# SyncE fetches one of 48 columns of source rows with single-row DMAs, and every edge pass gets six row buffers

## The chip, the cores and the metric

The kernel runs on one core of a Trainium2 chip. A core has five engines with an instruction stream each: TensorE (PE, with its weight loads as PEld), VectorE (DVE), ScalarE (ACT), GpSimd (POOL) and SyncE (SP), and 16 DMA engines that they share. SyncE computes nothing: it waits, works on registers and issues DMAs. The metric is device time in microseconds (us) from one launch, the median of several runs; lower is better. The kernel before took 13483.18 us (three runs, 13480.51 to 13506.48).

## The reference

A stack of four graph layers over 12,500 nodes and 200,000 edges, float32. Each layer takes rows of a node table by the source of every edge and reduces them over the edges that share a destination. Cut to what matters:

```python
def _transformer_conv(x, src, dst, edge_attr, ...):          # twice: passes c1, c2
    ke = k[src] + e
    score = jnp.sum(q[dst] * ke, axis=-1) / jnp.sqrt(...)
    smax = jax.ops.segment_max(score, dst, num_segments=n_nodes)
    a = jnp.exp(score - smax[dst])
    denom = jax.ops.segment_sum(a, dst, num_segments=n_nodes)
    out = jax.ops.segment_sum((a / denom[dst])[:, None] * (v[src] + e), dst, ...)

# three attention layers of 4 or 1 heads: passes c3 (with edge attributes), c4, c5
logits = leaky_relu(ax_s[:, row] + ax_t[:, col] + ae, 0.2)
w = jnp.exp(logits - seg_max[col].T)
out = segment_sum(w / denom[col] * x_proj[:, row], col)

z = h[src] + h[dst] + ef                                     # pass c6
mean, mean_sq = segment_sum(z, dst) / deg, segment_sum(z * z, dst) / deg
mx, mn = segment_max(z, dst), segment_min(z, dst)
```

## The kernel before, in words

Edges come sorted by destination. They are laid over 128 partitions, 1563 per partition (ET), so that one *column* is one edge of each partition, 128 edges in all. Sixteen columns (GW) are a *group*; there are 98 groups (NGRP), the last of 11 columns. Each of the six edge passes c1 to c6 goes once over all groups: `conv_edges` makes c1 and c2, `gat_edges` c3 to c5, `pna_edges` c6. Between the passes stand node stages (`n1` to `n5`, `f6`), and before them `begin`.

In every pass POOL fetches the source rows: for each column one indirect DMA takes 128 rows out of a node table in device memory, by the indices in column `srcs[:, g*GW+k]`, into the row buffer `y` (L741 in c1 and c2, L1767 in c3 to c5, L2200 in c6). A row is 256 bytes (`h_tab`, c1, c2, c6) or 288 bytes (`g_tab`, c3 to c5). The POOL code is written out in full, 1563 fetches to a pass; only the first 80 of c1 are issued in `begin` already (L415). `y` has six slots of a group each in c1 and c2 (NY = 6) and two in c3 to c6; before a group's fetches POOL waits until VectorE has read the group that had the slot (`weighted`, or `added` in c6). Slot 1 of six, where the short last group comes, counts its rows on two semaphores.

VectorE takes the groups in order. In c1 and c2 it spreads q over the edges with scans (L763), multiplies with the rows (L773, the first instruction that needs them), reduces, keeps running maxima, weighs the rows (L799, which frees the slot) and sums with scans (L806). In c3 to c5 the first reader is L1796, in c6 L2228. ScalarE makes exponentials, turns q and masks into scan order (L839, L841) and stores the summed rows.

SyncE issues what else is loaded. In c1 and c2, for each group, `operands` waits until the group two before it is weighted and its q turned (L715, L716), then issues `q_rows` (L706, 776 KB) and `edge_attrs` (L710, 256 KB in pieces of 128 bytes, 16 per partition). In c3 it issues the attributes of a group after the matmul that read the last ones (L1742), in c6 after `added` (L2179); in c4 and c5 it has nothing to do after the first load. Waits on each engine hold whatever stands behind them in that engine's own stream.

Of the kernel before, what the change touches and what calls it, by code (L numbers as in the profile page):

```python
# [19 lines left out]
I32 = mybir.dt.int32  # L20
ALU = mybir.AluOpType
# [3 lines left out]
P = 128  # L25
# [27 lines left out]
HALVED = (NGRP - 1) % NY  # L53
BLOCKS = [(c, min(8, NC - c)) for c in range(0, NC, 8)]
NBLOCK, NGOT, LAG = len(BLOCKS), 4, 3
assert NP_ >= N_NODES and EP >= N_EDGES and NBLK % 2 == 0 and NGRP % 2 == 0 \
    and EP % CH == 0 and GW // 2 < GL <= GW and NS > NC and NS % (2 * SC) == 0
# [44 lines left out]
def width(g):  # L102

    return GL if g == NGRP - 1 else GW

# [44 lines left out]
class Stage:  # L150
# [38 lines left out]
    def gather_halves(self, name, each):  # L189

        return [[self.dma(f"{name}{b}{part}", each - CUT * b * part) for part in range(2)] for b in range(2)]

    def row_slots(self, fills, cut=0):

        return [[self.dma(f"gathered_first_{slot}{part}", (8 if slot == HALVED else 16) * GW * n - cut * part)
                 for part in range(1 + (slot == HALVED))] for slot, n in enumerate(fills)]

# [13 lines left out]
def build(nc, a, out):  # L211
# [40 lines left out]

    def by_edge(t):
        return t[0:EP, :].rearrange("(p t) f -> p t f", p=P)
# [12 lines left out]
    def indexed(ap):  # L267
        return bass.IndirectOffsetOnAxis(ap=ap, axis=0)

# [30 lines left out]
    def begin(y, wq_t, bq, wk_t, bk, we_t):  # L300
# [4 lines left out]
        row_i, row = sb("row_i", [P, 1], I32), sb("row", [P, 1])  # L305
        node_i, node, upto = sb("node_i", [P, NS], I32), sb("node", [P, NS]), sb("upto", [P, NS])
# [26 lines left out]
        w_loaded, srcs_loaded = st.dma("w_loaded", 16 * len(loads)), st.dma("srcs_loaded", 16)  # L333
        ad_zeroed, h_stored, q_stored = st.dma("ad_zeroed", 16 * AD), st.dma("h_stored", 16), st.dma("q_stored0", 16)
        scattered = [st.dma(f"scattered{b}", 16 * sum(n for _, n in BLOCKS[b::2])) for b in range(2)]
        filled = [st.dma(f"zeros_stored{b}", 16 * len(range(b, NGRP, 4))) for b in range(4)]
        gathered = st.row_slots([1] * (NY - 1))
        chunk_got = st.dma_slots("chunk_got", 16 * (NS // 2))
# [10 lines left out]
            whole_t whole_pen""")  # L349

        with nc.Block(no_gpsimd_drain=True) as block:
            @block.sync
            def _(sp):
# [6 lines left out]
                sp.dma_start(prev_i[:], a["dst"][0:EP].rearrange("(p t) -> p t", p=P)).then_inc(dst_loaded.h, 16)  # L360
                sp.wait_ge(*zeroed(1))
# [19 lines left out]
                sp.dma_start(by_node(q_tab), q_rows[:]).then_inc(q_stored.h, 16)  # L381
                sp.wait_ge(*ad_zeroed(16 * AD))
# [191 lines left out]

            @block.tensor
# [94 lines left out]
    def conv_edges(tag, rows, first_y=None):  # L670
# [21 lines left out]
        gathered = st.row_slots([len(range(slot, NGRP, NY)) - (slot < ahead) for slot in range(NY)], CUT)  # L692
# [9 lines left out]
        with nc.Block(no_gpsimd_drain=True) as block:  # L702
            @block.sync
            def _(sp):
# [28 lines left out]
            def _(pool):  # L733

                nc.gpsimd.indirect_dma_start(q0[:], None, q_tab, indexed(dst0[:])).then_inc(q0_got.h, 16)
                for g in range(ahead, NGRP):
# [3 lines left out]
                    for k in range(width(g)):  # L740
# [9 lines left out]
            def _(v):  # L750
                def step(pc, slot, use):
# [18 lines left out]
                    for part in halves(gathered[slot], pc):  # L770
                        v.wait_ge(*part((use + (slot >= ahead)) * ((8 if slot == HALVED else 16) * GW) - missing(pc)))
# [928 lines left out]
    def gat_edges(tag, rows, bd=None):  # L1700
# [4 lines left out]
        y = st.sb("y", [P, 2, GW, TG])  # L1705
# [23 lines left out]
        gathered = st.gather_halves(f"gathered_{'first' if tag in ('c1', 'c2', 'c3') else 'later'}_", 8 * GW * HALF)  # L1729
# [8 lines left out]
        with nc.Block(no_gpsimd_drain=True) as block:  # L1738
            @block.sync
            def _(sp):  # L1740
# [5 lines left out]
                sp.dma_start(ad_raw[:], by_edge(ad_start)).then_inc(ad_loaded.h, 16)  # L1746
                if bd is not None:
                    for b in range(2):
                        edge_attrs(0, b, GW)
                    with sp.Fori(1, HALF - 1) as i:  # L1750
                        for b in range(2):
                            sp.wait_ge(*e_scored[b](i))
                            edge_attrs(i, b, GW)
# [5 lines left out]
            def _(pool):  # L1759
                nc.gpsimd.indirect_dma_start(g0[:], None, g_tab, indexed(dst0[:])).then_inc(g0_got.h, 16)  # L1760
                for g in range(NGRP):
                    b = g % 2
                    if g >= 2:
                        pool.wait_ge(*weighted[b](g // 2))
                        pool.nop(nofuse=True)
                    for k in range(width(g)):
                        nc.gpsimd.indirect_dma_start(y[:, b, k, :], None, g_tab, source(g, k))\  # L1767
                            .then_inc(gathered[b][k // H2].h, 16)
# [17 lines left out]
            def _(v):  # L1786
                def step(pc):
                    g, i, b, w = pc.n, pc.i, pc.b, pc.w
                    cols = bass.ds(pc.col, w)
                    ys = y[:, pc.slot, pc.lo:pc.lo + w]  # L1790
# [3 lines left out]
                    for part in halves(gathered[pc.slot], pc):  # L1794
                        v.wait_ge(*part(pc.load * (8 * GW) + 8 * GW - missing(pc)))
# [67 lines left out]
                with v.Fori(0, HALF - 1) as i:  # L1863
                    for b in range(2):
                        step(piece(i, b))
                for pc in LASTS:
                    step(pc)
# [277 lines left out]
    def pna_edges(tag, rows):  # L2145
# [4 lines left out]
        y, ea = st.sb("y", [P, 2, GW, D]), st.sb("ea", [P, 2, GW, D])  # L2150
# [16 lines left out]
        gathered = st.gather_halves(f"gathered_{'first' if tag in ('c1', 'c2', 'c3') else 'later'}_", 8 * GW * HALF)  # L2167
# [7 lines left out]
        with nc.Block(no_gpsimd_drain=True) as block:  # L2175
            @block.sync
            def _(sp):
# [3 lines left out]

                for b in range(2):
                    edge_attrs(0, b, GW)
                with sp.Fori(1, HALF - 1) as i:
                    for b in range(2):
                        sp.wait_ge(*added[b](i))
                        edge_attrs(i, b, GW)
# [5 lines left out]
            def _(pool):  # L2193
                for g in range(NGRP):
                    b = g % 2
# [434 lines left out]
```

## Time and profile before

| | |
|---|---|
| median of the runs | 13483.18 us |
| span of the profiled execution | 13480.4 us |
| POOL busy | 10010.5 us (74%) |
| DVE busy | 6813.4 us (51%) |
| ACT busy | 4134.7 us (31%) |
| source-row fetches | 9378 in six passes |

The profiled execution is its own run; its span leaves out what lies ahead of the first and behind the last instruction of the kernel, and is 2.8 us under the median of the runs. "Busy" leaves out the time between two instructions, in which POOL gets its next indirect DMA ready; that time is shown as "idle before", put down to "issue". DMA issues of SyncE aren't counted as busy, but the timeline shows each with its duration, under the engine name SPq. Lines L1 to L2629 are lines of the kernel before.

### The profile page before, as it was taken

What the parts mean: (1) busy time and instruction counts of PE and PEld (TensorE: products, weight loads), DVE (VectorE), ACT (ScalarE), POOL (GpSimd) and SP (SyncE); (2) the same over time, 40 slices, a digit from 0 to 9 for tenths busy, and PEclk for the clock granted to TensorE, in tenths of its full rate; (3) what the DMA queues carried; (4) which work ended last, traced back from release to release, by engine and by line L of the source; (5) the groups of instructions that cost most, each with busy time, mean ns of one, the idle gap of its engine ahead of it and who ended that gap; (6) DMA issues with size and microseconds to landing.
All of it is one profiled execution on the core that took longest, in us unless ns stands there. A gap on an engine that the chain in (4) does not pass through costs nothing. (4 is left out here: it accounts for less than half of the span.)

```text
span 13480.4 us, 46161 instructions
## 1 busy us (share of the span) xinstructions
PE 515.1 (4%) x1768; PEld 338.5 (3%) x1768; DVE 6813.4 (51%) x10542; ACT 4134.7 (31%) x4038; POOL 10010.5 (74%) x10585
## 2 busy tenths in 40 slices
PE   3000001100000300000010000000000000000001
PEld 1000000100000200000000000000000000000000
DVE  2787776477777433333333333343333335656566
ACT  4333333233333312222212222211111113666663
POOL 7777777777777677777777777777777776777775
PEclk9999999555555655555555555555555555555555
DMA  8444443344444222222212222222222222444443
GB/s 328 128 126 119 119 119 100 95 119 119 120 120 120 57 66 63 63 61 63 60 47 59 59 58 59 59 48 57 59 59 59 58 59 82 159 159 157 159 153 121
DMA packets 919562, 1312.58 MB, mean 97 GB/s; under 512 B 600892, under 2 KB 616404, under 8 KB 906113
## 3 DMA queue, kind: packets, MB, share of 16 engines
q0 software_dynamic: 341536, 381.76, 15.7%
q10 hardware_dynamic: 85680, 537.82, 10.2%
q1 hardware_dynamic: 492209, 391.76, 10.1%
q14 instruction: 123, 1.01, 0.0%
q8 instruction: 14, 0.23, 0.0%
HBM read 651.09 MB, written 659.48 MB: 97 GB/s over the span
## 5 line engine op out<-in xcount | busy, mean ns | idle before, releaser
L1767 POOL DMA_INDIRECT c_y<-g_tab,srcs x4689 | 4426.0, 944 | 1429.0 <-issue 1376.9
L2200 POOL DMA_INDIRECT c_y<-h_tab,srcs x1563 | 1474.8, 944 | 510.8 <-issue 466.5
L741 POOL DMA_INDIRECT c_y<-h_tab,srcs x1563 | 1474.9, 944 | 476.3 <-issue 476.3
L1796 DVE TENSOR_TENSOR c_s<-c_y,c_ad 128x64 f32<-128x64 f32 (+1 forms) x297 | 79.1, 266 | 3450.0 <-DMA c_y<-g_tab,srcs 3448.7
L741 POOL DMA_INDIRECT first_y<-h_tab,srcs x1483 | 1399.3, 944 | 452.9 <-issue 451.7
L1879 ACT ACTIVATE c_ex<-c_de 128x64 f32<-128x64 f32 (+1 forms) x297 | 67.4, 227 | 2321.1 <-DVE c_de L1827 2320.0
L1840 DVE TENSOR_TENSOR_SCAN c_acc<-c_r,c_w_in 128x1156 f32<-128x1156 f32 (+1 forms) x297 | 753.0, 2535 | 23.2
L763 DVE TENSOR_TENSOR_SCAN c_q_all<-c_mask,c_q_in 128x408 f32<-128x408 f32 (+2 forms) x792 | 734.0, 995 | 17.8 <-issue 10.5
L806 DVE TENSOR_TENSOR_SCAN c_acc<-c_r,c_w_in 128x408 f32<-128x408 f32 (+2 forms) x792 | 731.1, 986 | 8.2
L839 ACT ACTIVATE c_q_in<-c_q_raw 128x1552 f32<-128x1552 f32 (+1 forms) x198 | 596.2, 3011 | 195.8 <-DVE c_q_in L822 195.8
L1893 ACT ACTIVATE c_row<-c_acc 128x1088 f32<-128x1088 f32 (+1 forms) x297 | 617.7, 2080 | 0.0
L853 ACT ACTIVATE c_ex<-c_de 128x16 f32<-128x16 f32 (+1 forms) x198 | 37.1, 187 | 1842.2 <-DVE c_de L795 1842.2
L1833 DVE TENSOR_TENSOR c_w_in<-c_y,c_ex 128x1024 f32<-128x1024 f32 (+1 forms) x297 | 581.4, 1957 | 0.0
L867 ACT ACTIVATE c_row<-c_acc 128x1552 f32<-128x1552 f32 (+1 forms) x198 | 564.6, 2852 | 0.0
L2243 DVE TENSOR_TENSOR_SCAN c_acc_s<-c_mask,c_su 128x442 f32<-128x442 f32 (+2 forms) x495 | 477.5, 1031 | 121.5 <-ACT c_su L2325 121.5
L2228 DVE TENSOR_TENSOR c_su<-c_y,c_ea_ps 128x1024 f32<-128x1024 f32 (+1 forms) x99 | 184.7, 1866 | 663.4 <-DMA c_y<-h_tab,srcs 663.4
L1879 ACT ACT_TABLE_LOAD x96 | 123.2, 1283 | 1268.2 <-DVE c_de L1827 1268.2
L2249 DVE TENSOR_TENSOR_SCAN c_acc_m<-c_penm,c_mu 128x442 f32<-128x442 f32 (+2 forms) x495 | 474.8, 1024 | 0.0
L1892 ACT ACTIVATE c_row<-c_fm 128x64 f32<-128x64 f32 (+1 forms) x297 | 91.4, 308 | 1149.2 <-DVE c_acc L1840 1149.2
L2334 ACT ACTIVATE c_row<-c_acc_s 128x2048 f32<-128x2048 f32 (+1 forms) x99 | 374.1, 3779 | 141.9 <-DVE c_acc_s L2243 141.9
L2336 ACT ACTIVATE c_row<-c_acc_m 128x2048 f32<-128x2048 f32 (+1 forms) x99 | 374.3, 3781 | 85.2 <-DVE c_acc_m L2249 85.2
L773 DVE TENSOR_TENSOR c_prod<-c_y,c_q_all 128x1552 f32<-128x1552 f32 (+1 forms) x99 | 173.2, 1749 | 396.3 <-DMA c_y<-h_tab,srcs 396.3
(402 smaller groups left out, 6461.6 us busy)
## 6 DMA issues: line engine op xcount, KB each, us to landing
rows_d<-c_row ACTq DMA_DIRECT2D x97, 2048.0 KB, 6.9
rows_d<-c_row ACTq DMA_DIRECT2D x291, 576.0 KB, 2.9
rows_d<-c_row ACTq DMA_DIRECT2D x194, 784.0 KB, 3.4
c_q_raw<-q_start SPq DMA_DIRECT2D x194, 776.0 KB, 4.5
q_start<-first_y SPq DMA_DIRECT2D x97, 776.0 KB, 9.0
c_y<-g_tab,srcs POOLq DMA_INDIRECT x4689, 2.5
c_y<-h_tab,srcs POOLq DMA_INDIRECT x3126, 2.5
c_ea<-in_edge_attr SPq DMA_DIRECT2D x97, 512.0 KB
```

The source lines that it names most:

```text
L741: nc.gpsimd.indirect_dma_start(y[:, g % NY, k, 0:D], None, h_tab, source(g, k))\
L763: last = v.tensor_tensor_scan(flat(qs[:, lo:hi]), flat(mk[:, 0:hi - lo]), flat(q_cur[:, lo:hi]), 0.0, ALU.mult, ALU.add)
L806: last = v.tensor_tensor_scan(flat(ac[:, lo:hi]), flat(rr[:, 0:hi - lo]), flat(w_cur[:, lo:hi]), 0.0, ALU.mult, ALU.add)
L839: act.activation(narrow(q_in[:, pc.b], pc.w)[:, :, 1:pc.w + 1], q_raw[:, pc.slot, pc.lo:pc.lo + pc.w].rearrange("p t f -> p f t"), ACT.Copy)
L867: act.activation(row[:, b, 0:w, 0:F], narrow(acc[:, b], w)[:, :, 1:w + 1].rearrange("p f t -> p t f"), ACT.Copy).then_inc(row_ready[b].h, 1)
L1767: nc.gpsimd.indirect_dma_start(y[:, b, k, :], None, g_tab, source(g, k))\
L1833: v.tensor_tensor(w_heads[:, :, 0:JG, 1:w + 1], ys[:, :, 0:D].rearrange("p t (h j) -> p h j t", h=H), ex[:, :, 0:w].unsqueeze(2).to_broadc ...
L1840: v.tensor_tensor_scan(flat(ac), flat(rr), flat(w_cur), 0.0, ALU.mult, ALU.add).then_inc(summed.h, 1)
L1893: act.activation(row[:, b, 0:w, 0:F], narrow(acc[:, b], w)[:, :, 1:w + 1].rearrange("p f t -> p t f"), ACT.Copy).then_inc(row_ready[b].h, 1)
L2200: nc.gpsimd.indirect_dma_start(y[:, b, k, :], None, h_tab, source(g, k))\
L2243: last = v.tensor_tensor_scan(flat(ac_s[:, lo:hi]), flat(mk[:, 0:hi - lo]), flat(su_c[:, lo:hi]), 0.0, ALU.mult, ALU.add)
L2249: last = v.tensor_tensor_scan(flat(ac_m[:, lo:hi]), flat(pm[:, 0:hi - lo]), flat(mu_c[:, lo:hi]), 0.0, ALU.add, ALU.max)
```

## The change

Of every three groups the last column of the third (k = 15 of slots 2 and 5) is no longer fetched by POOL. SyncE fetches its 128 rows one by one. There are 32 such columns (NSYNC). A table `places_d` in device memory, made in `begin` from the sources by VectorE, holds the byte offsets of the rows, once for 256-byte rows and once for 288-byte rows. SyncE brings a column's 128 offsets into one row of a small SBUF tile `at`, reads them in pieces of 21 or 22 into registers (TENSOR_LOAD), and issues one DMA per row with the offset from a register. A column is cut in thirds (43, 43 and 42 rows); one third is issued for each group, behind that group's operands. `load_places` and `await_places` bring the next offsets in time; `whole_first` fetches the whole first column at the start of a pass, except in c1, where POOL has fetched groups 0 to 4 in `begin`. VectorE waits for a column's rows in `arrived`. In c3 to c6 the row buffer `y` grows from two slots to six, the loops are written over six groups instead of two, and SyncE gets such a loop in c4 and c5 too.

```diff
+EVERY, SYNC_K = NY // 2, GW - 1
+SYNC_SLOTS, NSYNC = [EVERY - 1, NY - 1], NGRP // EVERY
+THIRDS = [0, 43, 86, P]
+def by_pool(g):
+    return width(g) - (g % NY in SYNC_SLOTS)
+    class SyncRows:
+        def load_places(self, sp, n, b):
+            sp.dma_start(self.at[b:b + 1, :], places_d[bass.ds(n * 2 + b + self.table * NSYNC, 1), :])\
+                .then_inc(self.at_loaded.h, 16)
+        def await_places(self, sp, n, b):
+            sp.wait_ge(*self.at_loaded((n * 2 + b + 1 - self.first) * 16))
+        def third(self, sp, b, part):
+            lo, hi = THIRDS[part:part + 2]
+            mid = (lo + hi + 1) // 2
+            rows = self.tab.rearrange("n f -> (n f)").bitcast(U8)
+            for a_, z in ((lo, mid), (mid, hi)):
+                _, places = nc.values_load_multi_w_load_instructions(
+                    self.at[b:b + 1, a_:z], [mybir.EngineType.SP], min_val=0, max_val=(NP_ - 1) * 4 * self.width,
+                    skip_runtime_bounds_check_because="rows of src")
+                for p, place in zip(range(a_, z), places):
+                    sp.dma_start(self.y[p:p + 1, SYNC_SLOTS[b], SYNC_K, 0:self.width].bitcast(U8),
+                                 rows[bass.ds(place, 4 * self.width)].rearrange("(a n) -> a n", a=1))\
+                        .then_inc(self.got[b].h, 16)
+        def work(self, sp, n, j, more=True):
+            if j == 0:
+                self.third(sp, 0, 2)
+            elif j < EVERY + 1:
+                if j == 1:
+                    self.await_places(sp, n, 1)
+                    if more:
+                        self.load_places(sp, n + 1, 0)
+                self.third(sp, 1, j - 1)
+            elif more:
+                if j == EVERY + 1:
+                    self.await_places(sp, n + 1, 0)
+                    self.load_places(sp, n + 1, 1)
+                self.third(sp, 0, j - EVERY - 1)
+        def whole_first(self, sp):
+            if self.first == 0:
+                for part in range(EVERY):
+                    self.third(sp, 0, part)
+        def arrived(self, v, slot, n):
+            if slot in SYNC_SLOTS:
+                b = SYNC_SLOTS.index(slot)
+                v.wait_ge(*self.got[b]((n + 1 - (b < self.first)) * (16 * P)))
...
@@ begin, sync, vector @@
+                    sp.dma_start(src_i[:], a["src"].rearrange("(p t) -> t p", p=P)
+                                 [EVERY * GW - 1:EVERY * GW * NSYNC:EVERY * GW, :]).then_inc(src_loaded.h, 16)
+                for n in range(2):
+                    sp.dma_start(places_d[n * NSYNC:(n + 1) * NSYNC, :], places[:, n, :]).then_inc(places_stored.h, 16)
+                v.tensor_copy(src_f[:], src_i[:]).then_inc(vs.h, 1)
+                v.tensor_scalar(places[:, 0, :], src_f[:], 4.0 * D, None, ALU.mult).then_inc(vs.h, 1)
...
@@ conv_edges, sync @@
+                by_sync.begin(sp)
                 for j in range(NY):
...
                     q_rows(0, j, GW)
                     edge_attrs(0, j, GW)
-                with sp.Fori(1, NGRP // NY) as n:
+                    if j == 1:
+                        by_sync.whole_first(sp)
+                    if j:
+                        by_sync.work(sp, 0, j)
+                with sp.Fori(1, NGRP // NY - 1) as n:
                     for j in range(NY):
                         operands(n, j, GW)
+                        by_sync.work(sp, n, j)
+                for j in range(NY):
+                    operands(NGRP // NY - 1, j, GW)
+                    by_sync.work(sp, NGRP // NY - 1, j, False)
@@ conv_edges, gpsimd @@
-                    for k in range(width(g)):
+                    for k in range(by_pool(g)):
@@ gat_edges (pna_edges alike) @@
-        y = st.sb("y", [P, 2, GW, TG])
+        y = st.sb("y", [P, NY, GW, TG])
...
+                by_sync.whole_first(sp)
+                by_sync.work(sp, 0, 1)
+                for j in range(2, NY):
+                    operands(0, j, GW)
...
                 for g in range(NGRP):
-                    b = g % 2
-                    if g >= 2:
-                        pool.wait_ge(*weighted[b](g // 2))
+                    if g >= NY:
+                        pool.wait_ge(*weighted[g % 2]((g - NY) // 2 + 1))
```

On SyncE, at the head of c1's loop over six groups, there stood before (ISA rows are register arithmetic; `c_q_raw` is the q of a group, `first_y` the row buffer of c1):

```order
L726 ISA
L706 ISA
L706 DMA c_q_raw<-q_start 128x1552
L710 ISA
L710 DMA first_y<-in_edge_attr 128x16x32
L706 ISA
L706 DMA c_q_raw<-q_start 128x1552
```

and in the changed kernel, whose line numbers are its own (`c_at` is the tile with the offsets):

```order
L829 ISA
L804 ISA
L804 DMA c_q_raw<-q_start 128x1552
L808 ISA
L808 DMA first_y<-in_edge_attr 128x16x32
L309 TENSOR_LOAD c_at
L313 DMA first_y<-h_tab 1x256 x21
L309 TENSOR_LOAD c_at
L313 DMA first_y<-h_tab 1x256 x21
```

Between the attributes of one group and the q of the next now stand two register loads and 42 (in other groups 43) single-row DMAs.

On POOL, in c2, the fetches of the pass and what follows them stood before as:

```order
L735 DMA c_q<-q_tab,dst 128x97
L741 DMA c_y<-h_tab,srcs 128x64 x1563
L914 DMA c_got<-rows_d,fix_at 128x98
```

and now:

```order
L842 DMA c_q<-q_tab,dst 128x97
L848 DMA c_y<-h_tab,srcs 128x64 x1531
L1022 DMA c_got<-rows_d,fix_at 128x98
```

32 fetches went from the pass; c3 to c6 lose as many each, c1 31.

## Rows read from the trace of the kernel before

**Rows 1.** Page, costliest groups: busy, mean ns | idle before, what ended it.
```profile
L1767 POOL DMA_INDIRECT c_y<-g_tab,srcs x4689 | 4426.0, 944 | 1429.0 <-issue 1376.9
...
L741 POOL DMA_INDIRECT c_y<-h_tab,srcs x1563 | 1474.9, 944 | 476.3 <-issue 476.3
L1796 DVE TENSOR_TENSOR c_s<-c_y,c_ad 128x64 f32<-128x64 f32 (+1 forms) x297 | 79.1, 266 | 3450.0 <-DMA c_y<-g_tab,srcs 3448.7
```

**Rows 2.** POOL's waits: us in total, times, longest us.
```profile
POOL c_y L1767 <- DVE c_w_in L1833: 52.1, 171, 0.3
```

**Rows 3.** SyncE's timeline in c1: start us, us, instruction.
```profile
505.55 0.33 SPq L706 DMA_DIRECT2D c_q_raw<-q_start  x1
...
521.23 0.33 SPq L706 DMA_DIRECT2D c_q_raw<-q_start  x1
...
1918.75 0.33 SPq L706 DMA_DIRECT2D c_q_raw<-q_start  x1
1919.27 0.38 SPq L710 DMA_DIRECT2D first_y<-in_edge_attr  x1
```

**Rows 4.** The same in stage n2: v_b one row, skip_w 64 rows, wev 8 rows.
```profile
4500.71 0.28 SPq L1389 DMA_DIRECT2D n_w_agg<-in_L_gnn_v_b  x1
4501.03 1.12 SPq L1389 DMA_DIRECT2D n_w_self<-in_L_gnn_s_w  x2
...
4503.47 2.51 SPq L1389 DMA_DIRECT2D n_w_sk<-in_L_gnn_skip_w  x4
4506.03 0.59 SPq L1389 DMA_DIRECT2D n_bsk<-in_L_gnn_skip_b  x1
...
4508.91 5.41 SPq L1259 DMA_DIRECT2D n_wev<-in_gat_we  x16
```

**Rows 5.** SyncE at L706: duration ns min/median/max, first and last start.
```profile
L706 SPq MOVE c_q_raw<-q_start x180: 29/29/38, 473.6 to 4407.9; - x180
```

**Rows 6.** DMA issues of the page: count, KB each, median us to landing.
```profile
c_q_raw<-q_start SPq DMA_DIRECT2D x194, 776.0 KB, 4.5
...
q_tab<-n_qs SPq DMA_DIRECT2D x1, 97.0 KB, 1.6
```

**Rows 7.** SyncE's timeline at the start of c1.
```profile
388.67 0.33 SPq L706 DMA_DIRECT2D c_q_raw<-q_start  x1
389.05 0.43 SPq L710 DMA_DIRECT2D first_y<-in_edge_attr  x1
389.52 3.35 SPq L706 DMA_DIRECT2D c_q_raw<-q_start  x1
392.91 0.45 SPq L710 DMA_DIRECT2D first_y<-in_edge_attr  x1
```

**Rows 8.** The same at the start of c2.
```profile
2519.34 0.33 SPq L706 DMA_DIRECT2D c_q_raw<-q_start  x1
2519.72 0.43 SPq L710 DMA_DIRECT2D c_y<-in_edge_attr  x1
2520.19 4.04 SPq L706 DMA_DIRECT2D c_q_raw<-q_start  x1
```

**Rows 9.** DVE at L773: ns, first and last start us, forms.
```profile
L773 DVE TENSOR_TENSOR c_prod<-first_y,c_q_all x99: 457/1771/1773, 403.0 to 2252.5; 128x1552 f32<-128x1552 f32 x97, 128x776 f32<-128x776 f32 x1, 128x291 f32<-128x291 f32 x1
L773 DVE TENSOR_TENSOR c_prod<-c_y,c_q_all x99: 457/1771/1772, 2542.6 to 4482.2; 128x1552 f32<-128x1552 f32 x97, 128x776 f32<-128x776 f32 x1, 128x291 f32<-128x291 f32 x1
```

**Rows 10.** DVE's timeline, last group of c1, its first piece.
```profile
2244.38 0.95 DVE L773 TENSOR_TENSOR c_prod<-first_y,c_q_all 128x776 f32<-128x776 f32 x1
```

**Rows 11.** Windows in c3, c6: us, busy of PE, PEld, DVE, ACT, POOL; clock, DMA.
```profile
4900.00:6600.00 1700.00, 56.07 (x170) 42.57 (x170) 591.49 (x1278) 357.82 (x385) 1285.20 (x1362) 0.50 0.27 62
...
11500.00:13200.00 1700.00, 0.00 (x0) 0.00 (x0) 1023.48 (x1107) 1057.28 (x681) 1284.94 (x1363) 0.50 0.48 158
```

**Rows 12.** SyncE's attribute DMAs in c3 and c6: ns, first and last start us.
```profile
L1742 SPq DMA_DIRECT2D c_ea<-in_edge_attr x98: 323/333/1073, 4754.9 to 6641.1; - x98
L2179 SPq DMA_DIRECT2D c_ea<-in_edge_attr x98: 332/333/425, 11321.6 to 13246.6; - x98
```

More of the change, by code:

```diff
@@ L360, in _ @@
                 sp.dma_start(prev_i[:], a["dst"][0:EP].rearrange("(p t) -> p t", p=P)).then_inc(dst_loaded.h, 16)
+                with nc.allow_non_contiguous_dma("one column of src in three groups"):
+                    sp.dma_start(src_i[:], a["src"].rearrange("(p t) -> t p", p=P)
+                                 [EVERY * GW - 1:EVERY * GW * NSYNC:EVERY * GW, :]).then_inc(src_loaded.h, 16)
                 sp.wait_ge(*zeroed(1))
@@ L1746, in _, with operands @@
                 sp.dma_start(ad_raw[:], by_edge(ad_start)).then_inc(ad_loaded.h, 16)
+                by_sync.begin(sp)
+                def operands(n, j, w, more=True):
+                    i, b = n * (NY // 2) + j // 2, j % 2
+                    if bd is not None:
+                        sp.wait_ge(*e_scored[b](i))
+                        edge_attrs(i, b, w)
+                    if w == GW:
+                        if j == 1 or j == EVERY + 1 and more:
+                            sp.wait_ge(*weighted[b](i))
+                        by_sync.work(sp, n, j, more)
                 if bd is not None:
@@ L1749, in _ @@
                         edge_attrs(0, b, GW)
[L1750 to L1753, printed above, removed]
+                by_sync.whole_first(sp)
+                by_sync.work(sp, 0, 1)
+                for j in range(2, NY):
+                    operands(0, j, GW)
+                with sp.Fori(1, NGRP // NY - 1) as n:
+                    for j in range(NY):
+                        operands(n, j, GW)
+                for j in range(NY):
+                    operands(NGRP // NY - 1, j, GW, False)
+                if bd is not None:
                     for b in range(2):
@@ L2166, in pna_edges @@
         e_loaded = st.dma_slots("e_loaded", 16 * HALF)
[L2167 removed]
+        gathered, by_sync = st.pass_slots(), SyncRows(st, y, h_tab, D, 0)
         row_stored = st.store_slots("row_stored")
@@ L2180, in edge_attrs, with operands @@
                                  [:, bass.ds((i * 2 + b) * GW, w), :]).then_inc(e_loaded[b].h, 16)
+                def operands(n, j, more=True):
+                    i, b = n * (NY // 2) + j // 2, j % 2
+                    sp.wait_ge(*added[b](i))
+                    edge_attrs(i, b, GW)
+                    by_sync.work(sp, n, j, more)
+                by_sync.begin(sp)
                 for b in range(2):
                     edge_attrs(0, b, GW)
[L2184 to L2187, printed above, removed]
+                by_sync.whole_first(sp)
+                by_sync.work(sp, 0, 1)
+                for j in range(2, NY):
+                    operands(0, j)
+                with sp.Fori(1, NGRP // NY - 1) as n:
+                    for j in range(NY):
+                        operands(n, j)
+                for j in range(NY):
+                    operands(NGRP // NY - 1, j, False)
                 for b in range(2):
```

95 lines of the change are left out of this document (61 added, 34 removed).

## The prediction

> **What bounds the kernel now.** I read the page's costliest groups first. POOL's indirect DMAs stand at the top: 4689 fetches in c3 to c5 are 4426.0 us busy and 1429.0 us idle ahead, and nearly all of the idle is "issue", time in which POOL waited for nothing [rows 1]. One fetch so takes (4426.0 + 1429.0) / 4689 = 1.249 us, in c2 (1474.9 + 476.3) / 1563 = 1.248 us. The reader is to see that it is the same figure in passes with different rows, consumers and buffer counts. Then POOL's waits: the largest on VectorE is 52.1 us in 171 pieces of at most 0.3 us [rows 2], which is the usual issue gap under another name, so POOL never stood still for a buffer. VectorE waits 3448.7 us for the rows in c3 to c5 [rows 1]. In every pass POOL's issue rate sets the pace: 48 fetches to three groups, 48 x 1.248 = 59.9 us, 19.97 us a group. Other engines have room: VectorE is busy 591.49 us of 1700 in c3, 7.0 us a group over 85 groups, and 1023.48 in c6, 12.0 a group [rows 11]; in c1 it could do a group in 15.7 us, which shows at the start of the pass, where the rows of five groups are there already (505.55 to 521.23 us) [rows 3]. SyncE issues two DMAs a group in c1 and c2 and sleeps otherwise.
>
> **What the change takes away.** 32 fetches a pass, 31 in c1: 191 x 1.248 = 238.4 us. Three groups then cost POOL 47 x 1.248 = 58.7 us. That is the whole possible gain, 40 us a pass. The six buffers give nothing by themselves, since two were never waited for.
>
> **What it puts on SyncE.** A column must now leave SyncE every 58.7 us, and each row is an instruction. Cost of a row: sixteen DMAs of eight 256-byte rows took 5.41 us one behind the other, 0.338 each, the one-row DMA 0.32 to the next start (4500.71 to 4501.03), four of 64 rows (4506.03 - 4503.47) / 4 = 0.64 [rows 4]. A DMA with its offset in a register has a MOVE ahead of it [rows 5]. Between q and attributes late in c1 lie 1919.27 - 1919.08 = 0.19 us with two register instructions, at the pass's start, where there are none, 0.05 [rows 3, 7]; so 0.07 for the MOVE. A row is 0.41 us, between 0.39 and 0.71. I take 0.41, the eight-row series, because it is the only long one of small DMAs: 128 x 0.41 = 52.5 us.
>
> Six register loads, of 21 or 22 values. The trace shows none. They have to fetch from a memory and come back. Bounds: 0.07 us, as a register instruction, and 1.6, as the shortest DMA from issue to landing [rows 6]; if each value were fetched by itself, more (a rival below). I take the middle, 0.8: 4.8 us.
>
> The operands of three groups in c1 and c2: 0.90 us from the start of q to the end of the attributes [rows 3] and about 0.25 for register work and waits, 3 x 1.15 = 3.5 us; in c3 and c6 one DMA a group, 3 x 0.55 = 1.7. The DMA for the next offsets: 0.4.
>
> The loop now has 12 loads, 256 to 270 DMAs with a register and as many MOVEs, near 580 instructions. No loop in the trace is so long; what a jump back costs then I bound by 0 and a DMA's 2.5 us, and take 2.0 for six groups, 1.0 for a column.
>
> The last term is one that the trace does show. At the start of c1 the DMA behind the attributes took 3.35 us to issue instead of 0.33, in c2 4.04 [rows 7, 8]: SyncE stands until the attribute DMA, 2048 pieces of 128 bytes, is worked off. In the steady state nobody noticed, since the next DMA came 19 us later. Now a row DMA stands right behind the attributes in each group of c1 and c2. Stall 3.0 us a group, of which the load ahead of it hides 0.8: 3 x 2.2 = 6.6 us a column, between 0 (the queue takes small DMAs in between) and 3 x 3.7 = 11. In c3 and c6 the attributes are one long piece per partition, and the next DMA there is not held: 0.
>
> Sums for a column: c1 and c2 52.5 + 4.8 + 3.5 + 0.4 + 1.0 + 6.6 = 68.8 us; c3 and c6 52.5 + 4.8 + 1.7 + 0.4 + 1.0 = 60.4; c4 and c5 58.7. Against POOL's 58.7, SyncE becomes the bound in c1 and c2, is just over it in c3 and c6, and level in c4 and c5.
>
> The Trainium skill has two rules here that speak against the change. "Runtime: NRT & Kernel Launch", section "Instruction fetch mechanics", puts a register load at about 200 ns per register even in bulk (for loads from device memory), and "DMA: Bandwidth & Descriptors", section "Latency and other measured facts", gives a load a floor of about 600 ns. No run here shows either yet. By the floor alone the loads would be 1.2 us cheaper a column than in my sum, by 200 ns a register an estimate of 4.4 us a load and some 17,700 us for the kernel.
>
> **Why a late SyncE is felt.** q and attributes of a group stand in SyncE's stream behind the third that was issued with the group before. What is queued behind a third is the next group's q; ScalarE's turn waits for it, VectorE's scans for the turn, and POOL, six groups on, for VectorE. So in c1 and c2 the whole pass runs at SyncE's pace, 68.8 / 3 = 22.9 us a group.
> c1: SyncE starts at 389 and reaches group 93, the last with a third, 92 groups on; q lands after 4.5 us [rows 6] and some 7.5 us of turn and scan follow: 389 + 92 x 22.9 + 12 = 2508. Four groups at VectorE's own 15.7 make 2571. Before, the last group was multiplied at 2244.4 [rows 10]. +326 us. c1 suffers most, since its lead of five groups is lost.
> c2: whole_first and the next third stand ahead of group 2's q: 2519 + 5 + 1 + 4 x 19 = 2601, multiply at 2613, group 93 at 2613 + 91 x 22.9 = 4697, + 63 = 4760; before 4482.2 - 8.1 (the distance of the last two pieces in c1) = 4474 [rows 9, 10]. +286 us.
> c3: attributes of group 2 at 4755 + 77, group 93 at 4837 + 91 x 20.1 = 6666, four more at about 9 us: 6702, against POOL's old end, 4755 + 1563 x 1.249 + 3 = 6710 [rows 1, 12]. -8 us.
> c6: 11333 + 77 + 9, + 91 x 20.1 + 4 x 13 = 13300, against 13287 (last attribute DMA at 13246.6 [rows 12] plus two groups). +13 us.
> c4, c5: SyncE is level with POOL and nothing else hangs on it: -40 each.
> In begin, the strided load of 4096 single sources and three small VectorE steps lie beside POOL's placing DMAs; the fills it delays end long before they are needed: 0.
> Sum: 326 + 286 - 8 + 13 - 80 = +537 us. From the span, 13480.4 + 537 = 14017; with the 2.8 us by which the median lies above the span, 14020.
>
> **Rivals.**
> *SyncE has room.* Row 0.39, load 0.07, no stall, no refetch: c1 and c2 cost 49.9 + 0.4 + 3.5 + 0.4 = 54.2 us, under 58.7; all is hidden and 238 us are won: 13,245. With a row at 0.41, a load at 0.5, the refetch and still no stall, c1 and c2 cost 60.4 a column; the sums above then give +69 and +29 us, less 160: 13,420. For it: the margin of 6 us is real if every unknown falls low. Against it: the two held DMAs of rows 7 and 8. Even with every other unknown low, a stall of 3 us a group makes 63.1 us a column and, by the same sums, +152 and +105 us in c1 and c2, less 160 in the others: 13,580.
> *The loads fetch value by value.* At 0.14 us a value, two register instructions, a load is 3.0 us; c1 and c2 cost 75.4 a column (the stall is then hidden), c3 to c6 13.2 more than in my sum: 537 + 2 x 205 + 4 x 422 = +2630, 16,110. At 0.07 us a value it is near 14,680. It decides from about 0.04 us a value, where the other four passes stop winning. For it: 128 values a column all have to come in; against it, only that no row shows one. It is the mechanism of the skill's 200 ns a register.
> *Row DMAs are held like the 64-row ones.* 0.64 + 0.07 a row [rows 4] makes 91 us a column before anything else, over 19,000. Against it: the eight-row series was not held.
> *Gain and loss cancel.* SyncE at 63 us in c1 and c2 costs +80 each and the other four win 40 each: 13,483.
>
> **Chances.** SyncE is the bound of c1 and c2 by the stall, loads under a microsecond or little more (13,550 to 14,500): 0.46. Loads value by value (above 14,500): 0.27. SyncE has room: 0.20. Cancelled: 0.05. Row DMAs held: 0.02. What a measurement can't tell from no change is 0.2%, 27 us. Faster 0.20, same 0.05, slower 0.75. The range, 13,300 to 16,000, leaves out the best part of the case with room and loads above about 0.12 us a value. The likeliest case's own range is 13,550 to 14,500.
>
> **What would show it.** Right: SyncE without idle time in c1 and c2, its first row DMA behind each attribute DMA near 3 us; q 22 to 23 us apart; VectorE waiting for ScalarE's turn at L763, no longer for POOL's rows; POOL waiting for VectorE in c1 and c2 and not in c4 and c5; TENSOR_LOAD near 0.8 us. Wrong: SyncE idle behind each third and a pass 40 us shorter (room), a TENSOR_LOAD of several us (value by value), a row DMA other than 0.34 us, or the DMA behind the attributes at 0.33.

## The result, and the profile after

| | us, median | from | to | runs |
|---|---|---|---|---|
| kernel before | 13483.4 | 13480.5 | 13506.5 | 4 |
| changed kernel | 16525.6 | 16523.4 | 16535.7 | 4 |

The ratio is 1.2256 (95% interval 1.2239 to 1.2273): the change costs 3042 us, 23%. The profiled execution of the changed kernel has a span of 16522.5 us, 3042.1 more than before. The forecast was slower, 14,020 us, with a range up to 16,000. The direction was right; the size was far off, outside the range, and it belongs to the rival that had 0.27.

Where the time went is read first from POOL's rows, whose first and last start mark each pass (duration ns min/median/max, then first and last start in us):

```profile
L848 POOL DMA_INDIRECT first_y<-h_tab,srcs x1452: 938/944/962, 391.8 to 2770.9; - x182
L848 POOL DMA_INDIRECT c_y<-h_tab,srcs x1531: 938/944/995, 3146.8 to 5595.3; - x192
L1893 POOL DMA_INDIRECT c_y<-g_tab,srcs x4593: 938/944/1012, 5975.1 to 13375.3; - x200
L2339 POOL DMA_INDIRECT c_y<-h_tab,srcs x1531: 938/944/1006, 13651.7 to 16203.5; - x192
```

A fetch still takes 944 ns, and c1 and c2 have 31 and 32 fewer of them, but 1531 fetches of c2 are spread over 2448.5 us, 1.60 us each, where 1.248 was the pace [rows 1]. From the first fetch of one pass to that of the next (c1 from the start of the span, c6 to its end), worked out from the traces, the passes became longer by 625, 593, 430, 336, 345 and 713 us from c1 to c6: 3042 together; the prediction had +326, +286, -8, -40, -40 and +13. No pass won. The costliest groups say what POOL waits for (busy, mean ns | idle before, what ended most of it), against [rows 1]:

```profile
L1893 POOL DMA_INDIRECT c_y<-g_tab,srcs x4593 | 4333.7, 944 | 2351.7 <-issue 1361.3
L2339 POOL DMA_INDIRECT c_y<-h_tab,srcs x1531 | 1444.5, 943 | 1143.5 <-DVE c_su L2368 666.9
L848 POOL DMA_INDIRECT c_y<-h_tab,srcs x1531 | 1444.4, 943 | 1005.3 <-DVE c_w_in L907 547.2
...
L1923 DVE TENSOR_TENSOR c_s<-c_y,c_ad 128x64 f32<-128x64 f32 (+1 forms) x297 | 79.2, 267 | 2978.8 <-DMA c_y<-g_tab 2930.3
```

POOL's idle beyond its usual issue gap is new, and VectorE ends it. VectorE in its turn waited before for `c_y<-g_tab,srcs`, POOL's fetches; the name now is `c_y<-g_tab`, without `srcs`: SyncE's rows. The list of waits (us in total, times, longest us) shows the rhythm, and for c1, c2, c3 and c6 the queue behind SyncE, against [rows 2]:

```profile
DVE c_s L1923 <- DMA c_y<-g_tab: 2930.3, 65, 49.1
...
ACT c_q_in L947 <- DMA c_q_raw<-q_start: 2543.5, 187, 52.7
...
DVE c_q_all L870 <- ACT c_mask L949: 1913.5, 187, 49.6
DVE c_s L1928 <- PE c_ps_e L1907: 1504.2, 93, 22.4
...
DVE c_su L2368 <- ACT c_ea_ps L2455: 707.3, 93, 39.9
```

In c4 and c5 VectorE waits in long pieces of up to 49 us (32 in each pass), where before it waited some 12 us at each group (3450.0 us over 297 groups, [rows 1]): three groups pass together when a column is whole. In c1 and c2 the q of a group comes late, ScalarE turns it late, VectorE scans late. In c3 and c6 it is the attributes that come late, which stand in SyncE's stream behind the rows too: VectorE waits for the matmul (`c_ps_e`) and for ScalarE's copy (`c_ea_ps`) that take them in. SyncE itself hardly waits any more. Its wait for VectorE in c1 and c2, before and after:

```profile
SPq L706 <- DVE c_w_in L799: 3506.6, 192, 20.8
```

```profile
SPq L804 <- DVE c_w_in L907: 53.1, 4, 14.8
```

Its register loads, which the trace of before did not have (L309), and its timeline in c1 (start us, us, instruction; the loads are not listed there):

```profile
L309 SPq TENSOR_LOAD <-c_at x1146: 1783/4546/8532, 398.6 to 16247.3; - x191
```

```profile
1240.07 11.52 SPq L313 DMA_DIRECT2D first_y<-h_tab  x22
1251.92 0.36 SPq L804 DMA_DIRECT2D c_q_raw<-q_start  x1
1252.47 0.40 SPq L808 DMA_DIRECT2D first_y<-in_edge_attr  x1
1253.14 2.83 SPq L297 DMA_DIRECT2D c_at<-places_d  x1
1258.03 14.05 SPq L313 DMA_DIRECT2D first_y<-h_tab  x26
```

A load has a median of 4.5 us, against the 0.8 of the sum. The DMA right behind the attributes is held, 2.83 us, as the two of [rows 7, 8] were. A row, in a stretch of c4 without a load between:

```profile
L313 SPq MOVE c_y<-g_tab x22: 29/29/29, 9340.3 to 9347.0; - x22
L313 SPq DMA_DIRECT2D c_y<-g_tab x22: 224/225/399, 9340.4 to 9347.1; - x22
```

(9347.1 - 9340.4) / 21 = 0.32 us, MOVE included. Worked out over the loops of the trace, one column costs SyncE in us:

| pass | loads | rows | rest | column | predicted |
|---|---|---|---|---|---|
| c1, c2 | 25.1 | 45.0 | 8.3 | 78.4 | 68.8 |
| c3 | 27.2 | 42.5 | 3.9 | 73.6 | 60.4 |
| c4, c5 | 25.8 | 43.0 | 2.2 | 71.0 | 58.7 |
| c6 | 34.0 | 44.6 | 3.8 | 82.3 | 60.4 |

Above POOL's old 59.9 that is 18.5, 13.7, 11.1 and 22.4 us a column; times 31 columns 574, 425, 344 and 694, which is near what the passes grew by (c1 and c2 grew by 51 and 19 us more; by the prediction's account c1's part is its lost lead). So the passes do run at SyncE's pace, and the question is why a load costs 4.5 us, and in c6 more.

### The profile page after: what moved, and what is told of

Read it like the earlier page. It is cut to its first block and busy times, and to the rows that moved or that the text cites. A ratio compares the mean times of both kernels' runs of the same rounds, so it can differ in the third digit from the quotient of the medians.

```text
span 16522.5 us, 96230 instructions
## 1 busy us (share of the span) xinstructions
PE 514.6 (3%) x1768; PEld 337.3 (2%) x1768; DVE 6823.4 (41%) x10545; ACT 4119.8 (25%) x4038; POOL 9827.5 (59%) x10394
## 5 line engine op out<-in xcount | busy, mean ns | idle before, releaser
L1893 POOL DMA_INDIRECT c_y<-g_tab,srcs x4593 | 4333.7, 944 | 2351.7 <-issue 1361.3
L2339 POOL DMA_INDIRECT c_y<-h_tab,srcs x1531 | 1444.5, 943 | 1143.5 <-DVE c_su L2368 666.9
L848 POOL DMA_INDIRECT c_y<-h_tab,srcs x1531 | 1444.4, 943 | 1005.3 <-DVE c_w_in L907 547.2
L2455 ACT ACTIVATE c_ea_ps<-c_ea 128x1024 f32<-128x1024 f32 (+1 forms) x99 | 100.4, 1015 | 1376.0 <-DMA c_ea<-in_edge_attr 1376.0
```

The costliest lines, as they stand in the source:

```text
L848: nc.gpsimd.indirect_dma_start(y[:, g % NY, k, 0:D], None, h_tab, source(g, k))\
L1893: nc.gpsimd.indirect_dma_start(y[:, g % NY, k, :], None, g_tab, source(g, k))\
L2339: nc.gpsimd.indirect_dma_start(y[:, g % NY, k, :], None, h_tab, source(g, k))\
```

## The experiments

**What a register load costs.** In the changed kernel the first load of a column takes 1.9 us and the other five some 4.5 (in c6 two of them up to 8.5). They differ in where they begin in the tile (0; 22, 43, 65, 86, 107) and in what stands ahead of them. One kernel, bench_loads, measures loads by themselves.

```diff
@@ kernel before, c4, SyncE, ahead of the pass @@
+for lo, n in BENCH:          # 22 pairs of (begin, values)
+    for _ in range(3):
+        _, vs_ = nc.values_load_multi_w_load_instructions(at[0:1, lo:lo + n], [SP], ...)
+        for v_ in (vs_[0], vs_[-1])[:1 + (n > 1)]:
+            sp.dma_start(scrap, g_tab[bass.ds(v_, 256)]).then_inc(bench_got.h, 16)
+            sp.wait_ge(*bench_got(m))
```

> The kernel before, and in c4 a table of 22 register loads of SyncE, each three times, before the pass's SyncE work (it has none otherwise in c4), each followed by one or two single-row DMAs of 256 bytes to a scrap tile. Theory A (the place where a load begins in its tile decides its price per value): 22 values from offset 0 take 1.9 us as the first piece in the changed kernel, from offsets 22 and 43 4.5 us; among 2, 4, 8, 16 the table shows which boundary is the cheap one; 1, 2, 4, 8, 16, 22 values from 0 rise by about 0.085 us a value, from 1 by about 0.2. Theory B (the place in the program decides: the first load of a column is cheap because of what went ahead of it): all loads of 22 values take the same time here, 1.9 or 4.5 us, wherever they begin. Theory C (a fixed cost for each load, little for a value): 1 value costs nearly what 22 cost. Kernel time: the 66 loads take 0.1 to 0.3 ms at most beside POOL's fetches of c4, so 13,480 to 13,500 us.

Measured: 13480.95 us. The rows of eight of the pairs, in this order: (0, 1), (0, 4), (0, 16), (4, 16), (1, 16), (0, 22), (22, 22), (0, 24):

```profile
L1759 SPq TENSOR_LOAD <-c_at x3: 433/443/470, 6984.7 to 6988.7; - x3
L1759 SPq TENSOR_LOAD <-c_at x3: 466/473/474, 7016.2 to 7022.5; - x3
L1759 SPq TENSOR_LOAD <-c_at x3: 1133/1135/1136, 7036.9 to 7044.4; - x3
L1759 SPq TENSOR_LOAD <-c_at x3: 1137/1137/1491, 7248.3 to 7255.8; - x3
L1759 SPq TENSOR_LOAD <-c_at x3: 3435/3437/4427, 7259.4 to 7272.9; - x3
L1759 SPq TENSOR_LOAD <-c_at x3: 1784/1796/2384, 7048.2 to 7058.3; - x3
L1759 SPq TENSOR_LOAD <-c_at x3: 4642/4643/5569, 7129.8 to 7144.3; - x3
L1759 SPq TENSOR_LOAD <-c_at x3: 1584/1589/1591, 7211.8 to 7220.5; - x3
```

Theory A holds. Sixteen values from 0 or from 4 take 1.14 us, from 1 they take 3.44. Begun at a multiple of 4 values (16 bytes), four values cost (1135 - 473) / 3 = 221 ns together; begun elsewhere, each value costs (4643 - 3437) / 6 = 201 ns, to the end of the load, past every boundary. Twenty-four values from 0 are cheaper than twenty-two, as if the last two of the twenty-two came singly. Theory B falls: here nothing but the wait for a DMA stands ahead of each load, and 22 values from 0 still take 1.80 us, from 22 4.64. Theory C falls: 22 values cost at least four times what 1 costs.

**The changed kernel with cheap loads.**

```diff
@@ aligned16 @@
-THIRDS = [0, 43, 86, P]
+THIRDS = [[0, 20, 44], [44, 64, 84], [84, 104, P]]
-for a_, z in ((lo, mid), (mid, hi)):
+for a_, z in zip(cuts[:-1], cuts[1:]):
@@ aligned64 @@
+THIRDS = [[0, 16, 32, 48], [48, 64, 80], [80, 96, 112, P]]
```

> The changed kernel with the six register loads of a column begun at 0, 20, 44, 64, 84 and 104 (multiples of 4 values, 16 bytes) instead of 0, 22, 43, 65, 86 and 107. Theory A with 16 bytes as the boundary: all loads near 1.9 us, a column's loads 25 to 34 us become 11.4; c1 and c2 drop by 13.7 us x 32 columns each, c3 by 15, c4 and c5 come down to POOL's 58.7 us (-12), c6 by 14 to 22: 13,700 to 14,000 us. Theory A with 64 bytes as the boundary: only offsets 0 and 64 are cheap, 2.6 us a column less, near 16,020 us. Theory B (place in the program): nothing changes, 16,525 us within 20.

> The changed kernel with eight loads of 16 values a column, begun at multiples of 16 values (64 bytes). Theory A with either boundary: 16 x 0.085 = 1.4 to 1.6 us a load, 8 loads 11 to 13 us a column instead of 25 to 34: 13,700 to 14,000 us. Theory B, with the time per value that the later loads have (0.21 us): 8 x 3.3 = 26.4 us, no change, 16,400 to 16,700 us.

Measured: 13981.9 and 14089.4 us, one run each; the second is 89 us above the range expected for it. Loads of aligned16, then of aligned64:

```profile
L308 SPq TENSOR_LOAD <-c_at x1146: 1357/1478/3147, 398.5 to 13705.8; - x191
```

```profile
L308 SPq TENSOR_LOAD <-c_at x1528: 1130/1232/4577, 399.7 to 13816.2; - x191
```

Multiples of 16 bytes suffice: a load of aligned64 has a median of 1.23 us for 16 values, near the 1.14 of bench_loads, and a column's eight loads come to 10 to 11 us in c1 to c5, no less than aligned16's six (9 to 11). That aligned64 is 107 us slower comes mostly in c1, c2 and c6 (35, 19 and 40 us); why was not tried. 2544 us of the 3042 were the places where the loads begin, with pieces of 20 or 24 values instead of 21 or 22. In aligned16 c3, c4 and c5 are now 39 us shorter each than before, what the change had promised there; c1, c2 and c6 are 225, 193 and 200 longer.

**Half the loads, begun where the changed kernel begins them.**

```diff
@@ half_loads: changed kernel @@
 for a_, z in ((lo, mid), (mid, hi)):
+    if a_ == lo:
         _, places = nc.values_load_multi_w_load_instructions(...)
```

> The changed kernel with one register load for each third instead of two: the second half of each third uses the registers of the first half, so SyncE fetches wrong rows for 63 of 128 places (the right addresses are what is left out); the rows, their number and size stay. If the loads are the bound, a column loses the three loads at 22, 65 and 107, 3 x 4.5 = 13.6 us (c6 3 x 8.5 = 25): c1, c2 and c3 -430 us each, c4 and c5 down to POOL's pace, -380 each, c6 -500 to -750, so 13,700 to 14,000 us. If the loads only cover another wait (the stall behind the attributes, the fetching of the program), that wait comes out in their place: in c1 and c2 at least 3 x 2.8 us minus what is covered now, and the whole above 14,500 us.

Measured: 13987.9 us, within the first expectation. Three of the six loads gone do nearly the same as six made fast: 11.0 to 11.8 us of loads a column here, 9.1 to 10.8 in aligned16. In c1 to c5 the loads had covered little. In c6 they had covered a wait: its loads fell from 34.0 to 11.0 us a column, but its rows rose from 44.6 to 53.3. The next runs look for both.

**The stall behind the attributes.** In c1 and c2 the loop's attribute DMA brings 1 of 16 columns, once with cheap loads, once with those of the changed kernel.

```diff
@@ few_attrs: aligned16; slow_few: changed kernel @@
-    edge_attrs(n, j, w)
+    edge_attrs(n, j, w if isinstance(n, int) else 1)
```

> As aligned16 (13,982 us), and in the loop of c1 and c2 the attribute DMA brings 1 of 16 columns (128 pieces of 128 bytes instead of 2048); the other attributes are what is left out, the rest of the work stays. Theory (SyncE stands behind the attribute DMA): the DMA of the next addresses right behind it falls from 3.0 us to 0.3, the first row behind a load of 1.5 us from 1.6 to 0.23, and the rows held later go too: 5 to 7 us a column of 65.5, x 60 columns in c1 and c2, 13,580 to 13,700 us. Rival (what holds SyncE is the number of its row DMAs in flight, not the attributes): no change, 13,950 to 14,000 us.

> The changed kernel with its slow register loads, and in the loop of c1 and c2 the attribute DMA brings 1 of 16 columns (the other attributes are what is left out). The prediction counted a stall behind the attributes of 6.6 us a column in c1 and c2 on top of the loads. Theory (long loads hide most of the stall; only the DMA of the next addresses, one in each column, stands right behind the attributes): 2.8 to 3.5 us a column less, x 60, 16,310 to 16,360 us. Rival (the stall comes on top, as the prediction had it): 6 to 8 us a column, 16,050 to 16,170 us. Rival (nothing is held by the attributes here): 16,525 us within 20.

Measured: 13694.8 and 16397.7 us, one run each. The DMA of the next offsets, right behind the attributes, between 1000 and 2300 us; the changed kernel, then aligned16, few_attrs and slow_few:

```profile
L297 SPq DMA_DIRECT2D c_at<-places_d x17: 2420/2583/2910, 1020.4 to 2272.9; - x17
```

```profile
L297 SPq DMA_DIRECT2D c_at<-places_d x20: 2407/2656/3062, 1044.2 to 2287.4; - x20
```

```profile
L297 SPq DMA_DIRECT2D c_at<-places_d x20: 248/252/253, 1000.6 to 2141.1; - x20
```

```profile
L297 SPq DMA_DIRECT2D c_at<-places_d x18: 248/249/249, 1005.7 to 2296.5; - x18
```

So the stall is real: 2.4 us for the DMA right behind, and with cheap loads, which cover little, 5.2 us a column in all (65.5 and 66.2 to 60.1 and 61.2), 287 us for the kernel, within the theory's range. The rest of it lies in the first row behind the loads that stand right behind the attributes, 1.4 us on average in aligned16 and 0.37 in few_attrs; in the changed kernel, behind a load of 4.5 us, that row takes 0.31. With loads of 4.5 us the attributes cost 128 us, 2.4 us a column: what is left of the stall passes during the load. slow_few lies 38 us above its theory's range, because one load of each column got slower (the one that begins at 22, from 4.5 to 5.9 us; loads 25.1 to 26.2 us a column); why was not tried. The prediction's way to add the stall, on top, fails.

**c6.** In c6 of aligned16 a row costs 0.416 us, and a column 66.2.

```diff
@@ few_c6: aligned16, pna_edges @@
-    edge_attrs(i, b, GW)
+    edge_attrs(i, b, GW if isinstance(n, int) else 1)
@@ more_stores: aligned16, pna_edges, ScalarE @@
     act.dma_start(by_edge(rows)[:, bass.ds(pc.col, w), :], row[:, b, 0:w]).then_inc(row_stored[b].h, 16)
+    act.dma_start(by_edge(rows_d[2])[:, bass.ds(pc.col, w), :], row[:, b, 0:w, 0:TG]).then_inc(row_stored[b].h, 16)
```

> As aligned16 (13,982 us), and in the loop of c6 the attribute DMA brings 1 of 16 columns (the others are what is left out). In c6 of aligned16 a row costs 0.416 us instead of 0.34, 10.5 us a column lie in rows of about 1 us, most of them 30 to 39 rows behind the attribute DMA. Theory (the row DMAs queue up behind the half megabyte of the attributes): these rows go back to 0.34 us, the column from 66.2 to 56 to 58 us, below POOL's 58.7: 32 x 7.5 = 240 us less, near 13,740 us. Rival (the program's length or VectorE's work in c6 holds them): 13,950 to 14,000 us.

Measured: 13998.0 us, the rival's range. The theory fell: c6's attributes hold nobody, the column stays at 66.3 us. The timeline of that run gave the next one (start us, us, instruction), and six of SyncE's rows behind the store:

```profile
13329.75 8.20 SPq L312 DMA_DIRECT2D c_y<-h_tab  x14
...
13330.58 0.34 ACTq L2478 DMA_DIRECT2D rows_d<-c_row  x1
```

```profile
L312 SPq DMA_DIRECT2D c_y<-h_tab x6: 324/1020/1069, 13331.4 to 13336.3; - x6
```

One microsecond after ScalarE issues the 2048 KB store of a group's results, four of SyncE's row DMAs take 1.0 to 1.1 us each and a fifth 0.7, instead of 0.23, and then it is over. Over the whole pass of aligned16 three rows a group take more than 0.9 us (299 in 98 groups).

> As aligned16 (13,982 us), and in c6 ScalarE stores 136 of the 256 result values of every edge a second time, to a table that nobody reads any more: 1.1 MB a group beside the 2.1 MB of the store that is there. In c6 of aligned16 the row DMAs of about 1 us stand 1 to 6 us behind ScalarE's store of the group's results, 10.5 us of them a column. Theory (the big store holds SyncE's row DMAs while its pieces are fed to the queues): half as many again, 5 to 6 us a column more, x 32, 14,140 to 14,180 us. Rival (store and held rows only stand at the same place of a group): 13,970 to 14,000 us.

Measured: 14130.8 us, 149 more than aligned16 and 9 short of the expected range. In c6 a column went from 66.2 to 70.7 us, 4.5 of the 5 to 6 expected, and the rows over 0.9 us from 299 to 528. So stores of ScalarE's queue delay SyncE's small DMAs. At 4.5 us for 1.1 MB, the 2.1 MB of the store that is there would cost some 8.5 us a column, an estimate, and c6's column is 9 us longer than c3's: most of c6's excess is theirs. The long loads of c6 in the changed kernel go with the same store. There two of a column's six loads, those at 65 and 107, take 8.0 to 8.5 us, 62 in the pass, and in the trace each of the 62 has a store of ScalarE issued 0.4 to 1.8 us after its start, as here:

```profile
L309 SPq TENSOR_LOAD <-c_at x1: 8486/8486/8486, 15017.4 to 15017.4; - x1
```

```profile
15018.69 0.34 ACTq L2479 DMA_DIRECT2D rows_d<-c_row  x1
```

With those loads gone (half_loads) or short (aligned16) no load is long any more, and the rows over 0.9 us number 320 and 299 instead of 62. No run changes the stores under the slow loads, so that the store lengthens a load is read from the traces, not tried by itself.

**What the six buffers do alone, and versions that use SyncE where it has room.** six_buffers takes SyncE's rows away; gat_only is aligned16 with SyncE's column in c3, c4 and c5 alone; one_in_six adds one column in six groups in c1, c2 and c6, 32 rows behind each of four groups.

```diff
@@ six_buffers @@
-SYNC_SLOTS, NSYNC = [EVERY - 1, NY - 1], NGRP // EVERY
+SYNC_SLOTS, NSYNC = [], NGRP // EVERY
@@ gat_only: aligned16 @@
+CONV_SLOTS, GAT_SLOTS, MAX_SLOTS = [], [2, 5], []
@@ one_in_six @@
+CONV_SLOTS, GAT_SLOTS, MAX_SLOTS = [5], [2, 5], [5]
+QUARTERS = [[0, 16, 32], [32, 48, 64], [64, 80, 96], [96, 112, P]]
+if len(self.slots) == 1:
+    if j == 1:
+        self.await_places(sp, n, 1)
+        sp.nop(nofuse=True)
+    if 1 <= j <= 4:
+        self.third(sp, 1, j - 1)
+    if j == 4 and more:
+        self.load_places(sp, n + 1, 1)
+    return
```

> The changed kernel without SyncE's rows: POOL fetches all 16 columns of a group again, into six buffers in all passes, and setup still makes the table of addresses. The prediction's claim, that the six buffers give nothing by themselves since two were never waited for: 13,483 us within 20. Rival, that POOL gains from the longer lead (the waits at the ends of the passes): 13,440 to 13,460. Rival, that setup's new DMAs and steps cost something: 13,500 or more.

> SyncE fetches the column only in c3, c4 and c5, with the loads at multiples of 4 values; c1, c2 and c6 are left to POOL (six buffers stay). From the passes of aligned16 (POOL 1910.8 us from first to last fetch there in c3 to c5 instead of 1950.1 before): 3 x 39.3 = -118 us, so 13,365. Rival, that SyncE's rows in these passes disturb what follows (the waits at the end of a pass, the fetching of the longer program): 13,400 to 13,480. Rival, that a column on SyncE is still a hair too slow in c3 (57.1 us of 58.7): c3 gains nothing, 13,405.

> As gat_only, and in c1, c2 and c6 SyncE fetches one column in six groups instead of in three: 32 rows behind each of four of six groups, two loads of 16 values each. A group with rows costs SyncE 32 x 0.36 = 11.6 + 2 x 1.24 = 2.5 + operands and what is held behind the attributes 4 to 5 us, together 18 to 19 us, below POOL's 19.9, and two of six groups have none. Theory (SyncE is off the path once its sum is below POOL's): 16 x 1.248 = 20 us less in each of the three passes, 60 us less than gat_only, 13,305 us. Rival (rows issued ahead of a group's q delay VectorE's turn whatever the mean): 13,365 to 13,480 us. Rival (the rows held behind the attributes come to more than 5 us a group): c1, c2 or c6 longer than before, over 13,483.

| | us, median | runs | ratio to before, 95% interval |
|---|---|---|---|
| before, measured with them | 13481.2 | 13 | |
| six_buffers | 13483.5 | 10 | 1.0002 (0.9992 to 1.0011) |
| gat_only | 13364.6 | 4 | 0.9913 (0.9897 to 0.9930) |
| one_in_six | 13310.5 | 4 | 0.9874 (0.9857 to 0.9890) |

All three came out as expected to within 6 us. The buffers and the added work in setup cost and give nothing. one_in_six beats both kernels, by 171 us against before. Its POOL rows in c2 and c6 (duration ns, first and last start):

```profile
L869 POOL DMA_INDIRECT c_y<-h_tab,srcs x1547: 940/944/958, 2503.9 to 4433.9; - x194
...
L2360 POOL DMA_INDIRECT c_y<-h_tab,srcs x1547: 940/944/1014, 11165.8 to 13096.1; - x194
```

(4433.9 - 2503.9) / 1546 = 1.248 us: POOL's own pace again, with 16 fetches fewer. The held rows are still there, a row costs 0.40 to 0.41 us in c1 and c2, but SyncE has the time.

## Why the prediction was right and wrong

**The bound before and the gain.** Right. POOL's 1.248 us sets the pace, a column taken away is worth 39 to 40 us a pass, and SyncE has to stay below 58.7 us: c3 to c5 of aligned16, at 57 us a column, won 39 us each. That six buffers alone give nothing: right, shown.

**The step that failed: the six register loads.** The sum had 4.8 us a column, measured were 25 to 34. The step took the middle, 0.8 us, between a register instruction and the shortest DMA, and treated a load as one event whatever it carries. A load from these places costs 0.201 us for each value, some 4.5 us in all. 20 to 29 us more a column, 31 times a pass, is more than the whole miss of 2505 us; the rows (next point) give a part back. With cheap loads the kernel took 13,982 us, 38 from the forecast, but that is luck, errors that cancel: 9 to 11 us of loads instead of 4.8, rows 6 to 9 us a column cheaper in c1 to c5, and by pass +225, +193, -39, -39, -39 and +200 us, where the forecast had +326, +286, -8, -40, -40 and +13. The rival had the mechanism and the sign, but stopped at 0.14 us a value, 16,110 us, because its price was made from two register instructions. In the trace of before nothing showed a load, and the prediction said so; then a bound at 1.6 us "as the shortest DMA" was no bound for the sum, since it left the number of values, which the code did show, to a rival.

The Trainium skill, "Runtime: NRT & Kernel Launch", section "Instruction fetch mechanics", has about 200 ns a register, for loads from device memory. This load is from SBUF, and 4.64 us for 22 values agrees with it; begun at a multiple of 16 bytes, 22 values took 1.80 us, 0.08 a value, and there the measurement decides. "DMA: Bandwidth & Descriptors", section "Latency and other measured facts", puts a load's floor at about 600 ns; here one value took 0.43 us and four 0.47, less than that floor, and the measurement decides. The estimate of some 17,700 us that the prediction worked out from the page lay 7% above the result, closer than the forecast, 15% below it.

**Rows.** Predicted 0.41, bounds 0.39 to 0.71; measured 0.32 between starts, 0.33 to 0.35 with the held ones. The eight-row series was too dear by 0.02 and its MOVE was counted on top although a DMA of one row with its MOVE costs what the one-row DMA of [rows 4] did alone. The error is 7.5 to 10 us a column in the change's favour and hides over a third of the other one, in c6 a quarter.

**The stall.** The mechanism is right and shown, the DMA behind the attributes 2.6 us instead of 0.25. Its size, 6.6 us a column, compares with 5.2 in the kernel with cheap loads. With loads of 4.5 us it is hidden but for 2.4: two terms were added that lie beside each other.

**c3 and c6 alike.** Wrong. c6 costs 9 us a column more than c3. That c6's attributes hold nobody was right (few_c6). The step looked for what holds SyncE among SyncE's own DMAs only; ScalarE's stores delay it too, shown by storing part of the results a second time.

**Jump and refetch, 1.0 us a column.** After each of the 26 jumps back of c1's and c2's loops SyncE pauses 2.5 to 2.6 us, 1.3 a column; after a jump of the kernel before it was 0.12. The size is right. What sets it stays open: the loop of one_in_six, with 128 row DMAs instead of 256, pauses 0.2 us in c1 and 5.7 in c2.

**Why a late SyncE is felt.** Right. With 78.4 us a column the prediction's own formula gives 389 + 92 x 26.13 + 12 + 63 = 2868 for c1's last group, 624 later than [rows 10]. The trace has it there, and the pass grew by 625:

```profile
2869.72 0.95 DVE L881 TENSOR_TENSOR c_prod<-first_y,c_q_all 128x776 f32<-128x776 f32 x1
```

**The signs.** That c1 and c2 would lose was right even with cheap loads, 225 and 193 us; that c6 would hardly lose was not, 713 us in the changed kernel and 200 with cheap loads. c4 and c5 were to win 40 each and lost 336 and 345: the sum had put SyncE level with POOL, with no room for any error, and the loads alone were 21 us off. Of the signs, SyncE without idle time and VectorE waiting for ScalarE's turn came as said. q came 26 us apart instead of 22 to 23, no row DMA near 3 us stood behind the attributes (the DMA of the offsets did, 2.6), and POOL waited for VectorE in c4 and c5 too, 576.3 us in 48 pieces.

**Two of the rivals' figures.** "Gain and loss cancel" put the break-even at 63 us a column in c1 and c2, with +80 us each; by the sums of the rival above it, 63.1 us cost +152 and +105, so the break-even lay near 61.4. And by the prediction's own sums the upper end of the range, 16,000, is reached at about 0.135 us a value, not 0.12. Neither changes what was forecast.

## What to carry to other kernels

When a change adds an operation that the trace does not show, count what is inside it (values, rows, descriptors) and bound it per piece, not per instruction. A register load should begin at a multiple of four 32-bit values and carry a multiple of four; measured here, this alone was worth 2.5 ms. Work handed to an engine with room must fit that engine's time in every pass with a margin for DMAs that others hold: give it where there is room (c3 to c5 whole, the other passes half) and the gain appears as computed.

## What the runs showed of the hardware

- A register load of SyncE from SBUF: 0.43 us for 1 value, 0.64 for 2, 0.47 for 4, 0.69 for 8, 1.14 for 16, 1.59 for 24, 1.81 for 28 from offset 0; from an offset that is no multiple of 4 values 3.44 for 16 and 4.64 for 22. The times go up by 0.22 us for every four values in the first case and by 0.20 us for every value in the second.
- SyncE issues a single-row DMA with its offset in a register every 0.32 us, 128 of them in 41 us if nothing holds them.
- Behind a 256 KB DMA in 2048 pieces of 128 bytes the next DMA of the same engine takes 2.6 us instead of 0.25, and the stall costs 5.2 us over three groups where cheap loads stand between.
- After a 2048 KB store issued by ScalarE, in the group shown, four of SyncE's small DMAs took 1.0 to 1.1 us each and one 0.7, instead of 0.23; 1.1 MB stored besides raised the DMAs over 0.9 us from 299 to 528 in the pass.
- After a jump back in a loop of SyncE with 256 row DMAs it pauses 2.5 to 2.6 us, in the short loops of the kernel before 0.12.
